# First attention of a fused block: outputs turned by VectorE in 32x32 blocks and divided on GpSimd, one maxima transpose, all step orders rewritten

## The reference, cut to what matters

```python
# A: windowed self-attention, windows of 128 rows, shifted by 64
h = _ln(x) * (1 + sc_msa) + sh_msa
qkv = roll(h @ w_qkv + b_qkv, -64).reshape(B, 8, 128, 3, 16, 16)
o = softmax(q @ k.T / 4) @ v;  x = x + (roll(o, 64) @ w_so + b_so) * g_msa
# B: cross-attention to 77 context rows, only the 16 largest scores of a row are kept
h = _ln(x) * (1 + sc_mca) + sh_mca
x = x + (softmax(top_k(q @ k.T / 4, 16)) @ v_of_those @ w_co + b_co) * g_mca
# C: gated MLP, 256 -> 2 x 1024 -> 256
h = _ln(x) * (1 + sc_mlp) + sh_mlp
x = x + ((silu(a) * b) @ w_m2 + b_m2) * g_mlp
# D: second cross-attention with a full softmax over 77 modulated context rows
x = x + (softmax(q @ k.T / 4) @ v @ Wp + bp)
```

## Time and profile before

| | value |
|---|---|
| median of 3 timed runs | 1102.59 us (1102.4 to 1103.7) |
| the profiled execution, timed | 1102.51 us |
| its span in the trace | 1100.4 us |
| TensorE busy | 1027.1 us, 93% |
| VectorE busy | 824.9 us, 75% |
| ScalarE busy | 809.6 us, 74% |
| GpSimd busy | 686.9 us, 62% |
| granted TensorE clock, mean | 0.964 |

### The profile page before, as it was taken

How to read it: one execution, slowest core, us unless ns; L and a number is a source line. 1 busy time by engine, 2 the same in 40 slices (tenths; PEclk the granted TensorE clock), 3 DMA queues, 4 the chain that set the end, 5 groups by cost and what they waited for, 6 DMA issues and landing times.

```text
span 1100.4 us, 33659 instructions
## 1 busy us (share of the span) xinstructions
PE 1027.1 (93%) x11268; PEld 905.6 (82%) x11268; DVE 824.9 (75%) x4170; ACT 809.6 (74%) x1745; POOL 686.9 (62%) x1068
## 2 busy tenths in 40 slices
PE   5787599999999999999999999999999999998875
PEld 4575488888888888889898888888988889987763
DVE  2325888888888888888888888888888888887321
ACT  1215477888888888888888888888888888876652
POOL 1243644766777677666766666766766676667544
PEclk9868899999999999999999999999999999999996
DMA  8062000000000000000000000000000000000000
GB/s 289 16 148 18 16 7 7 7 12 12 11 12 13 11 7 7 11 12 12 12 12 11 12 13 11 12 12 12 5 8 12 12 11 12 7 7 7 6 5 15
DMA packets 33849, 23.16 MB, mean 21 GB/s; under 512 B 22979, under 2 KB 31427, under 8 KB 33168
## 3 DMA queue, kind: packets, MB, share of 16 engines
q1 hardware_dynamic: 33680, 21.02, 7.4%
HBM read 16.19 MB, written 4.83 MB: 19 GB/s over the span
## 4 chain that ended last, share of the span: by engine, by line
PE 84%; POOL 5%; issue 4%; DMA 2%; SPq 2%; ACT 2%; DVE 1%; POOLq 0%; DVEq 0%; ACTq 0%
PE ps L1239 20%; PE ps L1248 9%; PE ps L1104 8%; PE ps L1228 8%; PE ps L1217 7%; PE ps L1201 6%; PE ps L1192 4%; PE ps L1154 3%; PE ps L1093 3%; PE ps L1135 3%; PE ps L1166 3%; PE ps L1125 2%; PE ps L1115 2%; PE ps L1143 1%; PE ps L1174 1%
## 5 line engine op out<-in xcount | busy, mean ns | idle before, releaser
L1239 PE MATMUL ps<-hT_C,w_m_sb 128*128 128x128 f32 x2048 | 258.1, 277 | 0.8 <-DVE hidden_C L917 0.4
L1239 PEld LDWEIGHTS ps<-hT_C,w_m_sb 128*128 128x128 f32 x2048 | 241.2, 192 | 7.0 <-issue 6.7
L917 DVE SCALAR_TENSOR_TENSOR hidden_C<-ps,cols_sb,silu_C 128x128 f32<-128x128 f32 x256 | 85.8, 346 | 77.4 <-ACT silu_C L665 77.3
L665 ACT ACTIVATE silu_C<-ps,cols_sb 128x128 f32<-128x128 f32 x256 | 87.5, 367 | 61.0 <-PE ps L1239 56.5
L1248 PE MATMUL ps<-w_m_sb,hidden_C 128*128 128x256 f32 x512 | 123.0, 383 | 2.5 <-DVE hidden_C L917 2.5
L484 POOL TENSOR_TENSOR p_D<-scores_D,rc_D 128x616 f32<-128x616 f32 x64 | 77.0, 1224 | 71.2 <-DVE rc_D L888 71.2
L866 DVE MATCH_REPLACE8 scores_left_B<-mx_B,scores_left_B 128x77 f32<-128x77 f32 x512 | 108.5, 224 | 0.0
L862 DVE MATCH_REPLACE8 scores_left_B<-mx_B,scores_B 128x77 f32<-128x77 f32 x512 | 108.0, 225 | 0.0
L484 POOL TENSOR_TENSOR p_B<-p_B,rc_B 128x616 f32<-128x616 f32 x64 | 77.9, 1217 | 47.4 <-DVE p_B L874 46.5
L1248 PEld LDWEIGHTS ps<-w_m_sb,hidden_C 128*128 128x128 f32 x512 | 92.2, 190 | 14.0 <-DVE hidden_C L917 3.5
L452 POOL TENSOR_TENSOR scores_D<-scores_D,mx_D 128x616 f32<-128x616 f32 x64 | 78.5, 1226 | 37.1 <-DVE mx_D L894 35.8
(11 more groups left out here) (184 smaller groups left out, 2702.3 us busy)
## 6 DMA issues: line engine op xcount, KB each, us to landing
x_A<-in_x SPq DMA_DIRECT2D x64, 64.0 KB, 2.2
out<-y_D SPq DMA_DIRECT2D x64, 64.0 KB, 2.1
w_mod_sb<-in_w_mod SPq DMA_DIRECT2D x2, 1024.0 KB, 11.1
w_m_sb<-in_w_m SPq DMA_DIRECT2D x1, 2048.0 KB, 7.8
w_m_sb<-in_w_m SPq DMA_DIRECT2D x1, 1024.0 KB, 10.0
w_qkv_sb<-in_w_qkv SPq DMA_DIRECT2D x1, 768.0 KB, 6.6
w_gate_sb<-in_w_gate SPq DMA_DIRECT2D x1, 768.0 KB, 7.3
rows_sb<-in_rows SPq DMA_DIRECT2D x1, 768.0 KB, 8.6
```

The source lines that it names most:

```text
L665: sc.activation(SA[:, j, :], bank(f"C.up{j}")[:, 0:P], ACT.Silu, bias=col("bm1_a", j)).then_inc(sa_ok, 1)
L917: v.scalar_tensor_tensor(out=G[:, t % G_COPIES, j, :], in0=bank(f"C.up{j}")[:, P:2 * P], scalar=col("bm1_b", j), in1=SA[:, j, :], op0=ALU. ...
L1239: ins = mm(bank(f"C.up{j}")[:, half * P:(half + 1) * P], w_m1[:, k, m:m + P], HT["C"][:, t % HT_COPIES["C"], k, :], start=(k == 0), stop=( ...
```

## The change

The stage A chain behind `scores_a` is changed, and the order of all steps on all engines.

```diff
             def maxima_a(t, c):
-                at = c * 2 * P + HD
-                rows_of_max = MXA[:, at:at + 2 * (P - HD)].rearrange(...)[:, :, 0:3 * QUAD + 1:QUAD]
-                v.tensor_reduce(rows_of_max.rearrange("p j g -> p g j"),
+                v.tensor_reduce(MXA[:, :, :, c],
...
             def transpose_max(t):
-                for n in range(2 * KC):
-                    ins = nc.tensor.transpose(bank("A.mT")[:, n * P:(n + 1) * P], MXA[:, n * P:(n + 1) * P], ident[:])
+                nc.tensor.transpose(bank("A.mT")[:, 0:P], MXA[:].rearrange("p g j r -> p (g j r)"), ident[:]).then_inc(mt_ps, 1)
...
             def add_maxima(t):
-                v.tensor_tensor(QA[:], bank("A.mT").rearrange("p (c j q) -> p c j q", c=KC, j=2),
-                                QT["A"][:].unsqueeze(2).to_broadcast([P, KC, 2, P]), ALU.add).then_inc(qa_ok, 1)
+                for j in range(2):
+                    ins = v.scalar_tensor_tensor(out=QA[:, :, j, :], in0=bank("A.mT")[:, 0:P].unsqueeze(1).to_broadcast([P, KC, P]),
+                                                 scalar=mask2[:, j:j + 1], in1=QT["A"][:], op0=ALU.mult, op1=ALU.add)
+                ins.then_inc(qa_ok, 1)
...
             def weigh_values_a(t):
-                        ins = mm(bank("A.PV")[quad(q), m * P:(m + 1) * P], va[:, h, :],
-                                 PT["A"][:, g, (2 * c + j) * P:(2 * c + j + 1) * P], start=True, stop=True)
+                blocks = bank("A.PV").rearrange("p (c b m i) -> p c m b i", c=KC, b=ROWS, m=2)
+                            ins = mm(blocks[quad(q), c, m], va[:, HH * c + 2 * q + m, :],
+                                     PT["A"][:, q, at:at + P].rearrange("p (b i) -> p b i", b=ROWS), start=True, stop=True)
...
-            def outputs_a(t):        # ScalarE
-            def transpose_back(t):   # TensorE
-            def transpose_o(t):      # TensorE
-            def divide_a(t):         # VectorE
+            def turn_outputs(t):     # VectorE
+                dve.wait_ge(pv_ps["A"], t + 1)
+                if not first(t):
+                    dve.wait_ge(o_ok, t)
+                v.transpose(EV[:].rearrange("p n r -> p (n r)"), bank("A.PV")).then_inc(ev_ok, 1)
+                dve.wait_ge(ev_ok, t + 1)
+                v.reciprocal(RC["A"][:], EV[:, :, HD:HD + 1]).then_inc(rca_ok, 1)
+            def divide_a(t):         # GpSimd
+                pool.wait_ge(rca_ok, t + 1)
+                if not first(t):
+                    pool.wait_ge(ot_ok["A"], t)
+                g.tensor_tensor(O[:], EV[:, :, 0:HD], RC["A"][:].to_broadcast([P, HEADS, HD]), ALU.mult).then_inc(o_ok, 1)
+            def turn_back(t):        # VectorE
+                dve.wait_ge(o_ok, t + 1)
+                if not first(t):
+                    dve.wait_ge(y_ps["A"], t)
+                v.transpose(OT["A"][:].rearrange("p c q -> p (c q)"), O[:].rearrange("p n d -> p (n d)")).then_inc(ot_ok["A"], 1)
```

497 lines of the change are left out of this document (243 added, 254 removed), and 3 rows, old and new, of the table BANK.

## The result

The changed kernel takes **1040.7 us** (median of 4 runs, 1039.8 to 1043.7) beside 1103.14 us for the kernel before: a ratio of 0.9438, 95% interval 0.9416 to 0.946. The forecast was 1077 us, with a range from 1064 to 1094.

The account below looks back on a forecast made before the run. TensorE was taken to bound the middle: period 29.70 to 28.78 us, -25.8 over 28 periods. With -1.5 and +2 at start and end, span 1100.4 became 1075.1; 2.2 for the timed median gave 1077, range 1064 to 1094.

Parts of the forecast that it names:

- removed transposes: TensorE, each period: dropping transpose_back, transpose_o and three of four transpose_max saves 0.97 us.
- narrow group: TensorE, each body: four instead of five groups of blocks on 32-row or 32-column tiles, saving 0.20 us.
- built-in waits: TensorE before scores B, B's first transpose_p and up3: little cover for maxima and shared banks, 0.25 us a period, ends 0 and 0.6.
- chunks of 32 columns: TensorE's weigh_values_a writing PSUM in 32-column pieces: no added time taken, upper end +1.25 us a tile.
- two block transposes: Added VectorE work in stage A, priced at 0.682 and 0.425 us, 1.11 together; ends 0.55 and 2.2.
- load of x(4): Start: x of tile 4 issued behind D's set_up_flat and the MLP weights, delaying its statistics; +2 us, ends -6 and +8.
- The cover that was named: Start: GpSimd's set-up of D's values ends at 120 us and ScalarE's first weight copy waits for it, hiding most late-x delay.
- Start and end: Early and late bodies: 0.97 us less TensorE work each but more waiting, -1.5 us for all; tile 4's later load +2.
- Everything covered: Rival: no new waits in the middle and the start 5 us shorter, -41 us, 1062; chance 0.13.
- VectorE did not set the pace: Rival denied here: VectorE's in-order queue with 3.1 us of unusable waits makes the period 29.2, 1088 us; chance 0.14.
- the ring of the maxima: Rival: stage A's hand-overs come just in time, TensorE stops 1.9 us per body, period 30.4, 1122 us; chance 0.09.
- the values block did not grow: Rival denied here: column chunks double stage A's values block, period 29.8, no change, 1103 us; chance 0.04.

Follow-up runs that it names:

- the parent: Changed kernel with x of tile 4 loaded before D's round trip and the MLP weights, and GpSimd clearing D's padding before its multiplications: 1029.5 us.

## Why the prediction was right or wrong

**Right: the middle.** Period forecast 28.78, measured 28.62. The removed transposes carry it: from block start to block start, over twenty bodies, the changed kernel has 0.66 us less for `transpose_back` and `transpose_o` and 0.36 less at `transpose_max`, 1.02 for the 0.97 reckoned. But it took the new order to get all of that; in the old order the stage gave 0.75, by the wait at bank 6. The narrow group is 0.15 us, not 0.20. The built-in waits, taken as 0.25 us, are smaller: up0, in front of the first transposes of B, takes 1.01 us to the next start where an `up` block takes 0.89 elsewhere, so about 0.1. The chunks of 32 columns cost nothing: the values block of A is busy 40.1 us in 1024 matmuls in both kernels, at 279 ns. Over 25 periods -27.0 us were measured, where the forecast's 0.92 would give -23.

**Right: the operations.** The two block transposes take 0.715 and 0.434 us, where the rows of the same sizes gave 0.68 and 0.43; the two additions 0.479 each for 0.467, GpSimd's division 0.623 for 0.726. VectorE is at 25.45 us a period where 26.07 was forecast: 0.3 more than before and not 0.9, although the operations took what was reckoned. Busy time is a union, so more overlap may hide the difference; this was not taken apart. The estimate from the Trainium skill ("Vector Engine (DVE) Microarchitecture Reference", section 3.8, with the fixed costs of "VectorE: DVE Perf Modes", errata section) was 0.66 and 0.33 us: it was 0.05 and 0.10 too low, and the nearest row of the same size was the better guide. The rule of "GPSIMD Engine Reference", section 4.1, that elementwise work is about twice as slow on GpSimd, shows here as 0.623 us beside the 0.425 of the same product on VectorE, a factor of 1.5, paid by an engine that has 7.5 us of slack in a period.

**Right in kind: the load of x(4).** Forecast at +2 us with ends at -6 and +8; it cost 8.4 us in the profile and 7.7 in the medians, at its upper end, so the term was mis-sized by some 6 us, and against the direction of the whole miss. The cover that was named (ScalarE's first copy of the weights waits for GpSimd's set-up of D in both kernels) was there, and was worth 3.5 us more once both were moved. The step did not price the lower clock behind TensorE's wait (the 2.36 us for 1.28).

**Wrong: "Start and end".** The step reads: "the early and late bodies are shorter on TensorE by the same 0.97, but wait more: I take -1.5 for all." It took the idle time at both ends as given, 45.7 and 27.5 us, and asked only what less TensorE work does to it. But a new order of all steps moves those waits themselves. The rows were at hand: GpSimd's stand of 23.1 us for the round trip of B, with the divisor of tile 0 behind it, against a new list that has the round trip earlier and the wait later; and in the new list both exponentials of D side by side. The prediction took from the start only what the change makes later, not what it makes earlier. By spans the kernel came out 33 us below the forecast's 1075.1. The 25 periods of the middle have 4 of them, and 29 are in the start and the end as cut here, which were to give 2.3 us together (three periods, less 1.5, plus 2) and gave 31.4. By the runs:

| term of the change | us |
|---|---|
| middle: stage A | -18.7 |
| middle: new order (of it 25 x 0.15 = 3.8 one narrow group) | -8.3 |
| start: stage A in the old order | +2.3 |
| start: new order, B's round trip and GpSimd's wait for it | -10.3 |
| start: new order, load of x(4) | +8.4 |
| start: new order, the rest | -13.7 |
| end: stage A | -1.3 |
| end: new order, both halves of D together | -5.0 |
| end: new order, the rest | -11.8 |
| sum (spans 1100.4 and 1041.9) | -58.4 |

The two "rest" lines are differences, not runs, and each start term carries the 4 us by which profiles of one code differ; by the medians the pair at B's round trip was 13.6 and not 10.3 us. For the end, three things in the traces go with the rest, without an edit that isolates each: the waits before D's `transpose_h` and before `down` are 4.3 and 2.5 us shorter; a tile passes from scores A to its last residual in 175.9 us of steady running where the stage alone in the old order takes 180.5, so less is left to do when the last tile enters; and 13.5 us less of TensorE's work run at the lower clock. The rest of the start stays open: three waits of TensorE in the start of the old order with the new stage (7.2 us for GpSimd before the transposes of B's weights, 3.1 us before `project_v` for the key blocks, 2.9 us for the gate weights) are absent from the new one, but no run isolates any of them.

As bookkeeping, the new order's -16.8 us at the end are 10.3 of idle time and 6.5 of busy time (the lower clock's 13.5 us, halved, is 6.7); the -15.6 at the start are 8.8 and 6.8 (14.8 halved is 7.4). The Trainium skill counts in this manner ("TensorE: Matmul & The Clock Gate", section "HAM oscillation — how this bites in real kernels"): half of the throttled time is its extra wall time. By that rule the parent's 30.5 us at the lower clock would be worth 15 us; no run here comes near it. The spare products show that such a sum must not be read as cause: at the end the clock can be bought back for some 2 to 3.5 us, at the start for nothing that can be seen; that other engines set the pace there is likely, but shown only for the step from tile 3 to tile 4.

**The rivals.** "Everything covered" came nearest, at 1062, with the same error: beyond the middle it gave 8 us. VectorE did not set the pace, the ring of the maxima did not close, the values block did not grow. The fast side was bounded by TensorE's work in the middle plus small change at the ends, so the range could not hold the time.

## What to carry to other kernels

When a change reorders everything, the start and the end are not constants: list each long wait there (engine, releaser, what is queued behind it), find both in the new order, and price it in both directions; less than a third of the span held more than half of this gain. A late transfer costs where an in-order engine waits for it in front of other work, so moving either the transfer or the wait may be enough, and moving both may bring no more. A removed block may have been the cover of a wait: ask which bank the block behind it wants, and who still reads that bank. A step's place in TensorE's order also fixes when it wants its PSUM bank: three places cost 1.6 us a period here.

## What was not expected of the hardware

- TensorE's granted clock falls from 2.4 to 1.2 GHz behind its waits of a few microseconds and the blocks that follow take nearly twice their time (ten transposes 2.36 us for 1.28, a projection 2.05 for 1.10); spare products in the waits kept it up (mean 0.982 to 0.993), and the end was 1.9 to 3.5 us shorter, the start not.
- A product of 128x128 by 128x256 in f32 occupies TensorE for 0.43 us, as two records 0.22 us apart.
- Matmuls that write PSUM in chunks of 32 columns cost the same as those that write 128 in a row: 279 ns in both kernels, 1024 of them.
